# First FFN of a four-layer graph network: four buffers of each kind in the quantisation, and sums of magnitudes as two float32r passes

## The chip, the cores and the metric

One core of a Trainium2 chip runs the whole program in one launch. The metric is the device time of one execution in microseconds (us); of the kernel before it is the median of three runs.

## The reference, cut to what matters

The network alternates four graph layers with four feed-forward layers (FFN) on 625 nodes of 512 features. The change is in the first FFN, which takes the normalised rows x (625x512) and weights that are quantised to three values, scaled by group:

```
def _quantize_weight(w, group_size):           # group_size = 128, EPS = 1e-5
    wg = w.reshape(o, i // group_size, group_size)
    scale = mean(abs(wg), axis=-1, keepdims=True) + EPS
    wq = clip(round(wg / scale), -1.0, 1.0) * scale
gate = x @ quantized(w_gate).T                  # 512 -> 1408
up   = x @ quantized(w_up).T                    # 512 -> 1408
y    = (silu(gate) * up) @ quantized(w_down).T  # 1408 -> 512
```

So for each run of 128 input weights the sum of the magnitudes is needed in full precision, and a weight becomes its sign times the scale if twice its magnitude is over the scale, and 0 otherwise.

## The kernel before, in words

Each engine has its own stream of instructions, written out in order; semaphores join them. The 1408 hidden features are cut into three units u = 0, 1, 2 of 512, 512 and 384 (`WIDTHS`). A unit's three weight matrices lie in WR[(u+1) % 2], so that unit u+1 is loaded and quantised while unit u is multiplied. The load of a unit is queued on SyncE and waits until TensorE is done with the unit before the one it replaces (`weights_used`).

In unit u TensorE (the loop from L1079) does, for each m of the 128-wide parts of the unit, a wide projection with the gate weights and one with the up weights (`project_wide`, matmuls by L732; the first pair of unit 0 by `two_projections`, L1027, between the transposes of the last tiles). ACT takes Silu of the gate half (`gated`, L1739), DVE multiplies it with the up half (L2558). Each frees its PSUM slot; there are two wide slots. Then come five down projections (L1065), whose results DVE adds to the stream (L2176). PSUM slots of kind T, also two, take the sums of magnitudes.

The quantisation of unit u+1 (`quantized`, on each engine a generator) goes in groups: 128 input rows by the unit's width (`groups_of`: 12 groups of 512 columns for unit 1; 8 of 384 and 3 of 512 for unit 2). For one group:

- ACT writes the magnitudes (L1640) and the signs (L1641) of the weights into the buffers AW and SGN. It runs `deep // 2` groups ahead, and waits before it until the product of the group that held the buffer is done (`quant_ready`, L1638).
- TensorE multiplies the magnitudes with a matrix of ones, an fp32 matmul (L915), which sums over the 128 rows.
- ACT copies sum/128 + 1e-5 into SCL (L1651).
- DVE compares 2 x magnitude with the scale (L2402), and multiplies the result with the scale (L2404).
- POOL multiplies this with the sign, back into the weights (L2028). For unit 0 itself, earlier in the program, DVE does this too (L2407).

`deep` is the number of buffers: 3 in the quantisation of unit 0, 2 in those of units 1 and 2. `PACE` says how many groups stand behind each gate and each up projection: in unit 0 one and two, in unit 1 none in the first round (m = 0), then two and two. Each generator is made at a unit's start and advanced by `next(ahead)`.

Of the kernel before, what the change touches and what calls it, by code (L numbers as in the profile page):

```python
# [32 lines left out]
NEG = -1.0e30  # L33
# [154 lines left out]
def program(nc, a, out, loops):  # L188
# [3 lines left out]
    def sb(name, shape, dt=F32):  # L192
        return ctx.enter_context(nc.sbuf_tensor(name, shape, dt))

    def passing(name, shape, dt=F32):

        with nc.sbuf_tensor(name, shape, dt) as t:
            return t

    def sem(name):  # L200
        return ctx.enter_context(nc.semaphore(name))
# [8 lines left out]
    with ctx:  # L210
# [23 lines left out]
        EA2 = sb("EA2", [128, N])  # L234
        with nc.sbuf_tensor("MODW_high", [128, D], F32):
            HRT_HIGH = passing("HRT_HIGH", [128, 4, N + 1], F32R)
        MODW = sb("MODW", [128, 4, D])
        BR = sb("BR", [128, 3, D])
        CS = sb("CS", [128, C_END])
# [41 lines left out]
        HOT0 = passing("HOT0", [128, NT, 4 * P], F32R)  # L281
        with nc.sbuf_tensor("AR_parts", [128, HR_], F32):
            HR = passing("HR", [128, NT, HEADS0, 2, DH0], F32R)
        with nc.sbuf_tensor("AR_hot", [128, HR_ + 2 * NT * D], F32):
            HOT1 = passing("HOT1", [128, NT, 4 * P], F32R)
        with nc.sbuf_tensor("AR_blocks", [128, PR_ + NT * N], F32):
# [4 lines left out]
        def view(at, parts, *shape, dt=F32):  # L291
# [95 lines left out]
        COND4 = view(KT_ + 1905, 128, N)  # L387
        CT8 = view(V_, 8, N)
        ROW0 = [FIRST[:, D * b:D * (b + 1)] for b in range(4)]
        AW = [ROW0[0:3]] + 2 * [[MODW[:, b, :] for b in range(2)]]  # L390
        SGN = [ROW0[3:4] + [WR[:, 0, 1, 1024 + D * b:1024 + D * (b + 1)] for b in range(2)]] + 2 * [[MODW[:, 2 + b, :] for b in range(2)]]
        SCL = [[MODW[:, 0, :], BR[:, 2, :], FS_ROWS[:, 0:D]]] + 2 * [
            [BR[:, 1 + b, :] for b in range(2)]]

        ID = CS[:, C_ID:C_ID + 128]
        SEL = CS[0:8, C_SEL:C_SEL + D]
# [26 lines left out]
        y_ready = sem("y_ready")  # L423
        uv_ready, hr_split = sem("uv_ready"), sem("hr_split")
        terms_ready, row_part_ready = sem("terms_ready"), sem("row_part_ready")
        short_ids_ready, short_ids_out = sem("short_ids_ready"), sem("short_ids_out")
        ids_in = [sem(f"edge_ids_in_{b}") for b in range(2)]
        apart_ready, from_ready, hot_built = sem("apart_ready"), sem("from_ready"), sem("hot_built")
        diff_filled, diff_taken, score_ready = sem("diff_filled"), sem("diff_taken"), sem("score_ready")
        weighed_ready = sem("weighed_ready")  # L430
        scattered = sem("scores_scattered")
        sums_scattered = [sem(f"sums_scattered_{b}") for b in range(2)]
        clear_row_ready, sums_cleared = sem("clear_row_ready"), sem("sums_cleared")
        scores_cleared = sem("scores_cleared")
        keys_ready, totals_ready = sem("keys_ready"), sem("totals_ready")
        onehot_ready, onehot_used = sem("onehot_ready"), sem("onehot_used")
# [12 lines left out]
        head_weighed, prob_ready = sem("head_weighed"), sem("prob_ready")  # L449
        relu_ready = sem("relu_ready")  # L450
        bias_added = sem("bias_added")
        absw_ready, kept_ready, quant_ready = sem("absw_ready"), sem("kept_ready"), sem("quant_ready")
        layer_ready = sem("layer_ready")
        value_rows_free = sem("value_rows_free")
# [34 lines left out]
        def loads(sp):  # L489
# [35 lines left out]
                    sp.dma_start(ER[g % 4][lo:hi].rearrange("p a b -> p (a b)"),  # L525
                                 a["edge_attr"][lo:hi, 256 * g:256 * (g + 1)]).then_inc(edge_in[g % 4], 16)

            sp.wait_ge(clear_row_ready, 2)
            for b in range(2):
                sp.dma_start(pair_sums[b].rearrange("(p q) c -> p (q c)", p=128)  # L530
                             .rearrange("p (a q) -> p a q", a=2),
                             FLAT[1].unsqueeze(1).broadcast_to([128, 2, 3053])).then_inc(sums_cleared, 16)
            sp.wait_ge(short_ids_ready, 1)
            for r in range(2):
                sp.dma_start(short_ids[r].rearrange("(m q) -> m q", q=P), SHORT_IDS[:, r, :])\
                  .then_inc(short_ids_out, 16)
# [173 lines left out]
        def _(pe):  # L710
# [199 lines left out]
            def quantized(u):  # L910

                for k, (j, c, width) in enumerate(groups_of(u)):
                    g = fill("T")
                    pe.wait_ge(absw_ready, n.add(absw_ready))
                    mm(g.ap[:, 0:width], ONES[:, :], AW[u][k % len(AW[u])][:, 0:width], start=True, stop=True)\  # L915
                        .then_inc(g.filled, 1)
                    yield

            ahead = quantized(0)
# [581 lines left out]
        def _(act):  # L1501
# [131 lines left out]
            def quantized(u):  # L1633
                def magnitudes(k):

                    j, c, width = groups[k]
                    if done[0] + k >= deep:
                        act.wait_ge(quant_ready, done[0] + k - deep + 1)  # L1638
                    w = wm((u + 1) % 2, j)[:, c, 0:width]
                    fn(AW[u][k % deep][:, 0:width], w, ACT.Abs).then_inc(absw_ready, 1)  # L1640
                    fn(SGN[u][k % deep][:, 0:width], w, ACT.Sign)  # L1641

                groups, deep = groups_of(u), len(AW[u])
                act.wait_ge(loaded[(u + 1) % 2], n.now(loaded[(u + 1) % 2]) + 48)
                for k in range(deep // 2):
                    magnitudes(k)
                for k, (j, c, width) in enumerate(groups):
                    if k + deep // 2 < len(groups):
                        magnitudes(k + deep // 2)
                    s = take("T")  # L1650
                    fn(SCL[u][k % deep][:, 0:width], s.ap[:, 0:width], ACT.Copy, bias=1e-5, scale=1.0 / 128)\  # L1651
                        .then_inc(s.taken, 1)
                    if k == len(groups) - 1:
                        done[0] += len(groups)
                    yield
# [78 lines left out]
            def gated(m, tiled=False):  # L1734
                s = take("W")
                if tiled:
                    fn(SG[m % 2].rearrange("p (c n) -> p c n", c=NT), by_tile(s), ACT.Silu).then_inc(s.taken, 1)
                else:
                    fn(SG[m % 2], s.across[:, :], ACT.Silu).then_inc(s.taken, 1)  # L1739
# [3 lines left out]
                fn(XT[:, :, tile(t)], s.ap[:, 0:4 * P].rearrange("p (c n) -> p c n", c=K4), ACT.Copy)\  # L1743
                    .then_inc(s.taken, 1)

            transpose_y()
            for u in range(3):
                n.add(loaded[(u + 1) % 2], 48)
                ahead = quantized(u + 1) if u < 2 else iter(())
                for m in range(WIDTHS[u] // 128):  # L1750
                    pace = PACE[u][min(m, 1)]
                    gated(m, tiled=(u == m == 0))
                    for _ in range(pace[0]):
                        next(ahead, None)
                    psum.skip(W=1)
                    for _ in range(pace[1]):
                        next(ahead, None)
                psum.skip(N=NT)
# [367 lines left out]
        def _(dve):  # L2126
# [54 lines left out]
                dve.wait_ge(s.taken, n.now(s.filled))  # L2181


            v.memset(FLAT[1], 0.0).then_inc(clear_row_ready, 1)
            v.memset(FLAT[0], NEG).then_inc(clear_row_ready, 1)
            v.memset(TS[:, :, :], 0.0)
            v.memset(CW[:, :, :], 0.0)
            v.memset(CWP[:, :, 0:1], 1.0)
# [3 lines left out]
            dve.wait_ge(start_done, 10)  # L2192
            dve.wait_ge(index_in, 48)
            v.tensor_copy(SHORT_IDS[:, 0, :], SRC_ROWS)
            v.tensor_copy(SHORT_IDS[:, 1, :], DST_ROWS).then_inc(short_ids_ready, 1)
            v.scalar_tensor_tensor(KEYT, SRC_ROWS, float(N), DST_ROWS, ALU.mult, ALU.add).then_inc(keys_ready, 1)
            v.reduce_max(SM[0:ET, 0:1], WEIGHT_ROWS, AX.X).then_inc(layer_ready, 1)
            dve.wait_ge(keys_ready, 1)
# [195 lines left out]
                    ALU.mult).then_inc(uv_ready, 1)  # L2394
            def quantized(u):

                for k, (j, c, width) in enumerate(groups_of(u)):
                    s = psum.next("T")
                    dve.wait_ge(s[0].taken, s[1])
                    deep = len(AW[u])  # L2400
                    w, z = AW[u][k % deep][:, 0:width], SCL[u][k % deep][:, 0:width]
                    step(v.scalar_tensor_tensor(w, w, 2.0, z, ALU.mult, ALU.is_gt))  # L2402
                    if u:
                        v.tensor_tensor(z, z, w, ALU.mult).then_inc(kept_ready, 1)  # L2404
                    else:
                        step(v.tensor_tensor(z, z, w, ALU.mult))
                        v.tensor_tensor(wm(1, j)[:, c, 0:width], z, SGN[0][k % deep][:, 0:width], ALU.mult)\  # L2407
                         .then_inc(quant_ready, 1)
                    yield
# [153 lines left out]

            psum.skip(T=NT)
            v.tensor_scalar(MASK[:, :, :], CNT[:, :, :], 0.5, -NEG, ALU.is_lt, ALU.mult)
            for u in range(3):
                ahead = quantized(u + 1) if u < 2 else graph_weights()
                for m in range(WIDTHS[u] // 128):
                    pace = PACE[u][min(m, 1)]
                    s, k, _ = psum.next("W")  # L2570
                    for _ in range(pace[0]):
                        next(ahead, None)
                    b = take("W")
                    dve.wait_ge(s.taken, k)
                    gated(m, b, tiled=(u == m == 0))
                    for _ in range(pace[1]):
                        next(ahead, None)
                if u < 2:
                    for t in range(NT):
                        add_to_stream(t, take("N"))  # L2580
                else:
                    followed(streamed, norm_y)
# [522 lines left out]
```

## Time and profile before

| | us |
|---|---|
| median of three runs | 2250.25 |
| lowest and highest | 2247.23, 2251.97 |
| profiled execution | 2255.45 |
| its span | 2253.6 |
| TensorE matmuls busy | 2119.1 (94%) |
| DVE, ACT, POOL busy | 1024.7, 710.9, 551.3 |
| mean granted clock of TensorE | 0.972 |

In the profile, PE is TensorE, PEld its weight loads. An fp32 matmul stands as two instructions, and spans of pipelined matmuls overlap, so the cost of one is read from start to start. A tile is named by the tensor it lies in: AR is the large arena, WR the weights, MODW and BR are small tensors that the quantisation borrows for its buffers.

### The profile page before, as it was taken

How to read it: one execution, taken by the hardware profiler on the slowest of the kernel's cores; microseconds unless marked ns; L12 is line 12 of the kernel's file. 1: busy time of each engine (PE TensorE's matmuls, PEld its weight loads, DVE VectorE, ACT ScalarE, POOL GpSimd, SP SyncE). 2: the span in 40 equal slices, each digit the busy share in tenths (PEclk: the TensorE clock that was granted, in tenths of full speed). 3: DMA queues.
4: the chain of work that ended last, by engine and by line, in shares of the span. 5: the costliest groups of instructions: out<-in, count | busy, mean ns of one | idle time of the engine just before them, and what ended most of it. 6: DMA issues, size and time to landing. Idle time of an engine off the chain costs nothing.

```text
span 2253.6 us, 21932 instructions
## 1 busy us (share of the span) xinstructions
PE 2119.1 (94%) x8162; PEld 1276.7 (57%) x8162; DVE 1024.7 (45%) x2159; ACT 710.9 (32%) x1191; POOL 551.3 (24%) x467
## 2 busy tenths in 40 slices
PE   5899887898889999998999999999999999999998
PEld 3577564787456565554565565565565544444443
DVE  8898677686334324356445355255355300000002
ACT  1477565675231110012242242252251111111110
POOL 4678763453220101012003003002102200122202
PEclk9999999799999789999999999999999899999999
DMA  9522213631112102111011011010101677778832
GB/s 345 178 32 32 27 14 76 171 90 60 41 58 75 38 19 86 43 75 61 15 57 62 19 57 42 30 51 24 53 9 48 246 294 291 295 303 300 300 128 74
DMA packets 61507, 237.47 MB, mean 105 GB/s; under 512 B 23343, under 2 KB 28419, under 8 KB 39276
## 3 DMA queue, kind: packets, MB, share of 16 engines
q1 hardware_dynamic: 31898, 168.25, 20.7%
q0 software_dynamic: 26336, 62.19, 9.0%
q10 hardware_dynamic: 3168, 5.63, 0.7%
q8 instruction: 66, 1.08, 0.2%
q14 instruction: 39, 0.32, 0.0%
HBM read 204.06 MB, written 31.96 MB: 105 GB/s over the span
## 4 chain that ended last, share of the span: by engine, by line
PE 77%; DVE 12%; issue 4%; POOL 3%; ACT 3%; DMA 2%; ACTq 0%; DVEq 0%; POOLq 0%
PE PS L739 10%; PE PS L1027 10%; PE PS L732 9%; PE PS L1420 7%; PE PS L1429 7%; PE PS L1458 7%; PE PS L883 3%; PE PS L1065 3%; PE PS L1306 2%; PE PS L1223 2%; PE PS L1326 2%; PE PS L1327 2%; PE PS L750 1%; PE PS L1205 1%; DVE AR L2436 1%
## 5 line engine op out<-in xcount | busy, mean ns | idle before, releaser
L1984 POOL TENSOR_TENSOR RSTD<-VE,HALF 125x1 f32<-125x1 f32 x100 | 81.1, 811 | 972.5 <-DVE VE L2154 972.5
L1027 PE MATMUL PS<-XT,WR 128*128 128x500 f32 (+2 forms) x992 | 233.5, 392 | 8.4 <-ACT XT L1526 4.4
L883 PE MATMUL PS<-HR,HOT 125*125 125x512 f32 x800 | 211.8, 413 | 16.4 <-DVE HOT L2298 14.9
L2991 DVE TENSOR_TENSOR AR<-AR,PS 128x512 f32<-128x512 f32 (+1 forms) x44 | 30.3, 688 | 404.3 <-PE PS L1429 404.3
L739 PE MATMUL PS<-WR,XT 128*125 128x512 f32 (+1 forms) x464 | 205.5, 590 | 0.6 <-DVE AR L2775 0.3
L1027 PEld LDWEIGHTS PS<-XT,WR 128*128 128x128 f32 x992 | 144.7, 193 | 87.9 <-issue 72.5
L883 PEld LDWEIGHTS PS<-HR,HOT 125*125 125x125 f32 x800 | 147.0, 192 | 58.3 <-DVE HOT L2298 17.2
L2002 POOL DMA_INDIRECT pair_sums<-CW,SIDX x80 | 136.2, 1702 | 54.1 <-DMA pair_sums<-CW,SIDX 21.9
L739 PEld LDWEIGHTS PS<-WR,XT 128*125 128x125 f32 x464 | 86.9, 193 | 89.0 <-issue 85.0
L732 PE MATMUL PS<-XT,WR 128*128 128x313 f32 (+3 forms) x432 | 120.7, 436 | 1.8 <-DVE CW L2262 1.3
L1943 ACT ACTIVATE AR<-PS 128x512 f32<-128x512 f32 (+1 forms) x44 | 26.3, 597 | 299.0 <-PE PS L1420 299.0
L2176 DVE TENSOR_TENSOR AR<-PS,AR 125x512 f32<-125x512 f32 x55 | 38.0, 691 | 178.9 <-PE PS L739 107.3
L732 PEld LDWEIGHTS PS<-XT,WR 128*128 128x128 f32 (+1 forms) x432 | 82.9, 193 | 40.6 <-issue 9.9
L2013 POOL DMA_INDIRECT pair_scores<-TS,SIDX x80 | 88.6, 1107 | 63.0 <-DMA pair_scores<-TS,SIDX 47.5
L732 PE MATMUL PS<-AR 128*125 128x313 f32 (+3 forms) x360 | 101.5, 435 | 0.0
L1526 ACT ACTIVATE XT<-PS 128x500 f32<-128x500 f32 x60 | 35.3, 590 | 209.5 <-PE PS L750 209.5
L1458 PE MATMUL PS<-AR,MODW 128*128 128x512 f32 (+1 forms) x192 | 86.4, 593 | 0.7 <-ACT MODW L1932 0.7
L732 PEld LDWEIGHTS PS<-AR 128*125 128x125 f32 (+1 forms) x360 | 61.1, 187 | 33.9 <-DVE DEN L2813 14.8
L739 PE MATMUL PS<-WR,AR 128*125 128x512 f32 (+1 forms) x200 | 76.6, 530 | 1.7 <-ACT AR L1917 0.9
L2298 DVE SCALAR_TENSOR_TENSOR HOT<-AR,NODE,WR 125x500 fp32r<-125x500 int16 x100 | 71.1, 731 | 7.0 <-ACT WR L1558 6.1
L2319 DVE TENSOR_REDUCE TS<-WR 125x8 f32<-125x512 f32 x80 | 54.4, 680 | 40.3 <-DMA pair_scores<-TS,SIDX 40.3
L1458 PE MATMUL PS<-WR,MODW 128*128 128x512 f32 (+1 forms) x160 | 71.9, 592 | 0.0
(427 smaller groups left out, 3874.2 us busy)
## 6 DMA issues: line engine op xcount, KB each, us to landing
WR<-in_qkv SPq DMA_DIRECT2D x12, 1024.0 KB
WR<-in_omm SPq DMA_DIRECT2D x12, 1024.0 KB
pair_scores<-CNT SPq DMA_DIRECT2D x1, 12212.0 KB
AR<-pair_scores SPq DMA_DIRECT2D x5, 2187.5 KB
AR<-in_x_a SPq DMA_DIRECT2D x10, 1024.0 KB, 9.8
AR<-in_x_b SPq DMA_DIRECT2D x10, 1024.0 KB, 4.9
AR<-in_x_c SPq DMA_DIRECT2D x10, 1024.0 KB, 7.3
WR<-in_x_a SPq DMA_DIRECT2D x8, 1024.0 KB, 8.9
```

Source lines behind the costliest of these rows:

```text
L732: last = mm(s.across[0:parts, c0:c1], lhs(k), rhs(k)[:, c0:c1], start=(k == 0), stop=(k == terms - 1))
L739: last = mm(s.ap[0:P, 0:cols], lhs, rhs, start=(k == 0), stop=(k == len(pairs) - 1))
L883: last = mm(DIFF[m % 4], HOT[g % 2][0:P, k, tile(j)], HR[0:P, k, :, b, :], start=(k == 0 and b == 0), stop=(k == NT - 1 and b == 1))
L1027: last = mm(by_tile(s)[:, t0:t1, :], w[:, k, 128 * m:128 * (m + 1)], XT[:, k, P * t0:P * t1].rearrange("p (c n) -> p c n", n=P), start=(k ...
L1065: last = mm(o.ap[0:P, :], HT[:, m, tile(t)], w[:, m, :], start=(m == 0), stop=(m == len(chunks) - 1))
L1420: last = mm(bank(2 + k % 2, rows_of(k)), stationary(k, c), w[:, c, :], start=(c == 0), stop=(c == K4 - 1))
L1429: last = mm(bank(4 + k % 2, rows_of(k)), stationary(k, c), w[:, c, :], start=(c == 0), stop=(c == K4 - 1))
L1458: last = mm(bank(6 + n % 2, rows), HTX[k % 2][:, c, 0:rows], w[:, c, :], start=(u == 0 and c == 0), stop=((is_shared(k) or u == 1) and c = ...
L1984: g.tensor_tensor(RSTD[:, t:t + 1], VE[:, t:t + 1], HALF[:, :], ALU.pow)\
L2002: g.indirect_dma_start(out=pair_sums[m % 2], out_offset=bass.IndirectOffsetOnAxis(ap=SIDX[:, m:m + 1], axis=0), in_=CW[:, m, :], in_offset ...
L2013: g.indirect_dma_start(out=pair_scores, out_offset=bass.IndirectOffsetOnAxis(ap=SIDX[:, m:m + 1], axis=0), in_=TS[:, m % SCORES_AHEAD, :], ...
L2298: v.scalar_tensor_tensor(HOT[g % 2][0:P, k, :], IDB[g // 2 % 2][0:P, 1, 500 * (g % 2):500 * (g % 2 + 1)], NODE[:, 0, k:k + 1], FROM[q % 4] ...
```

## The change

For the quantisation of units 1 and 2 there are now four buffers of each kind, in the arena, and so ACT runs two groups ahead. ACT writes the magnitudes twice, once in full and once rounded to float32r (the high part); DVE subtracts the rounded from the full one (the low part); TensorE sums both parts into one PSUM slot by two float32r passes in place of the fp32 matmul. Each generator gets a first step of its own that prepares two groups: for unit 1 it is taken on ACT after the third of five transposed tiles and on DVE after the mask, for unit 2 at the start of unit 1's second round, ahead of its Silu and gated product. Two semaphores of the program's start are merged into one.

```diff
+        HIGH_PARTS = passing("HIGH_PARTS", [128, 4, D], F32R)
...
+        with nc.sbuf_tensor("AR_low", [128, 8192], F32):
+            LOW_PARTS = passing("LOW_PARTS", [128, 4, D], F32R)
...
-        AW = [ROW0[0:3]] + 2 * [[MODW[:, b, :] for b in range(2)]]
-        SGN = [ROW0[3:4] + [...]] + 2 * [[MODW[:, 2 + b, :] for b in range(2)]]
+        AW = [ROW0[0:3]] + 2 * [[view(XL_ + D * b, 128, D) for b in range(4)]]
+        SGN = [ROW0[3:4] + [...]] + 2 * [
+            [view(at, 128, D) for at in (10240, 10752, 11264, 12640)]]
         SCL = [[MODW[:, 0, :], BR[:, 2, :], FS_ROWS[:, 0:D]]] + 2 * [
-            [BR[:, 1 + b, :] for b in range(2)]]
+            [BR[:, b, :] for b in range(3)] + [view(XL_ + 4 * D, 128, D)]]
...
# TensorE
-                    mm(g.ap[:, 0:width], ONES[:, :], AW[u][k % len(AW[u])][:, 0:width], start=True, stop=True)\
-                        .then_inc(g.filled, 1)
+                    if u:
+                        for part_ in (HIGH_PARTS, LOW_PARTS):
+                            last = mm(g.ap[:, 0:width], ONES[:, :].bitcast(F32R), part_[:, k % 4, 0:width],
+                                      start=(part_ is HIGH_PARTS), stop=(part_ is LOW_PARTS))
+                    else:
+                        last = mm(g.ap[:, 0:width], ONES[:, :], AW[u][k % len(AW[u])][:, 0:width],
+                                  start=True, stop=True)
+                    last.then_inc(g.filled, 1)
...
# ACT
-                    fn(AW[u][k % deep][:, 0:width], w, ACT.Abs).then_inc(absw_ready, 1)
+                    if u:
+                        fn(AW[u][k % deep][:, 0:width], w, ACT.Abs)
+                        fn(HIGH_PARTS[:, k % deep, 0:width], w, ACT.Abs).then_inc(rounded_ready, 1)
+                    else:
+                        fn(AW[u][k % deep][:, 0:width], w, ACT.Abs).then_inc(absw_ready, 1)
...
                 for k in range(deep // 2):
                     magnitudes(k)
+                if u:
+                    yield
...
-            transpose_y()
+            for t in range(3):
+                turned_row(t)
+            ahead = quantized(1)
+            next(ahead)
+            for t in range(3, NT):
+                turned_row(t)
             for u in range(3):
                 n.add(loaded[(u + 1) % 2], 48)
-                ahead = quantized(u + 1) if u < 2 else iter(())
                 for m in range(WIDTHS[u] // 128):
                     pace = PACE[u][min(m, 1)]
+                    if u == m == 1:
+                        ahead = quantized(2)
+                        next(ahead)
                     gated(m, tiled=(u == m == 0))
...
# DVE
+                def low_part(k):
+                    width = groups[k][2]
+                    dve.wait_ge(rounded_ready, n.add(rounded_ready))
+                    v.tensor_tensor(LOW_PARTS[:, k % 4, 0:width], AW[u][k % 4][:, 0:width],
+                                    HIGH_PARTS[:, k % 4, 0:width].bitcast(F32), ALU.subtract).then_inc(absw_ready, 1)
+                if u:
+                    low_part(0)
+                    low_part(1)
+                    yield
+                for k, (j, c, width) in enumerate(groups):
+                    if u and k + 2 < len(groups):
+                        low_part(k + 2)
...
             v.tensor_scalar(MASK[:, :, :], CNT[:, :, :], 0.5, -NEG, ALU.is_lt, ALU.mult)
+            ahead = quantized(1)
+            next(ahead)
             for u in range(3):
-                ahead = quantized(u + 1) if u < 2 else graph_weights()
+                if u == 2:
+                    ahead = graph_weights()
                 for m in range(WIDTHS[u] // 128):
                     pace = PACE[u][min(m, 1)]
+                    if u == m == 1:
+                        ahead = quantized(2)
+                        next(ahead)
                     s, k, _ = psum.next("W")
```

## Rows read from the trace of the kernel before

**Rows 1.** The page, part 4: the chain that ended last, by engine.
```profile
PE 77%; DVE 12%; issue 4%; POOL 3%; ACT 3%; DMA 2%; ACTq 0%; DVEq 0%; POOLq 0%
```

**Rows 2.** The chain in order of time (start us, us, what), one group in unit 0.
```profile
552.26 1.27 POOL WR L2028
553.56 0.63 ACT MODW L1640
554.19 0.52 ACT MODW L1641
554.71 0.49 ACT BR L1651
555.23 0.70 DVE MODW L2402
555.95 0.70 DVE BR L2404
556.72 1.28 POOL WR L2028
```

**Rows 3.** Busy time by stretch: length, PE, PEld, DVE, ACT, POOL, clock, DMA.
```profile
547.50:595.40 47.90, 37.58 (x128) 23.05 (x127) 16.73 (x25) 21.64 (x39) 12.65 (x10) 1.00 0.00 0
613.00:663.10 50.10, 42.82 (x150) 27.97 (x151) 13.72 (x23) 17.46 (x36) 9.23 (x9) 1.00 0.28 111
```

**Rows 4.** The timeline of PE in units 0 and 1 (start us, us, engine line).
```profile
555.27 4.37 PE L732 MATMUL PS<-XT,WR 128*128 128x312 f32 x16
559.48 1.02 PE L915 MATMUL PS<-MODW,ONES 128*128 128x512 f32 x2
560.34 4.37 PE L732 MATMUL PS<-XT,WR 128*128 128x312 f32 x16
...
595.42 17.33 PE L1065 MATMUL PS<-WR,AR 128*125 128x512 f32 x40
613.01 12.86 PE L732 MATMUL PS<-XT,WR 128*128 128x312 f32 x48 [0.27 <-issue]
...
663.13 17.33 PE L1065 MATMUL PS<-WR,AR 128*125 128x512 f32 x40
```

**Rows 5.** The timeline of PE in the first graph layer: ten float32r matmuls.
```profile
200.10 2.58 PE L883 MATMUL PS<-HR,HOT 125*125 125x512 f32 x10
202.52 0.39 PE L894 MATMUL PS<-Y,WR 125*128 125x512 bf16 x1
```

**Rows 6.** Operations that write float32r: a group of ACT, one of DVE.
```profile
L1664 ACT ACTIVATE HRT_HIGH<-PS 128x500 fp32r<-128x500 f32 x5 | 3.0, 594 | 0.8 <-PE PS L925 0.8
490.68 0.68 DVE L2426 TENSOR_TENSOR LEFT<-PS,LEFT 128x500 fp32r<-128x500 f32 x1
```

**Rows 7.** The timelines of DVE and POOL where they meet.
```profile
596.87 1.65 POOL L2028 TENSOR_TENSOR WR<-BR,MODW 128x512 f32<-128x512 f32 x1 [3.20 <-DVE BR L2404]
663.82 0.80 DVE L2558 TENSOR_TENSOR AR<-AR,PS 128x625 f32<-128x625 f32 x1
663.98 1.27 POOL L2028 TENSOR_TENSOR WR<-BR,MODW 128x512 f32<-128x512 f32 x1 [3.19 <-DVE BR L2404]
664.54 1.26 DVE L2402 SCALAR_TENSOR_TENSOR MODW<-MODW,BR 128x512 f32<-128x512 f32 x1
```

**Rows 8.** DMA rate in 40 slices of 526 to 542 us, and 612 to 628.
```profile
GB/s 0 0 0 20 164 123 246 430 492 389 369 492 410 410 430 430 410 389 492 389 369 512 410 389 338 139 0 20 13 13 0 0 0 0 0 0 0 41 0 0
GB/s 0 0 0 0 164 266 123 348 430 369 512 430 369 492 369 451 451 369 410 369 471 389 430 471 380 21 257 115 115 189 95 142 95 142 95 142 95 189 47 237
```

**Rows 9.** The timeline of ACT: a tile copy, and the Silu of two rounds.
```profile
541.85 0.59 ACT L1526 ACTIVATE XT<-PS 128x500 f32<-128x500 f32 x1 [3.48 <-PE PS L750]
547.48 0.69 ACT L1737 ACTIVATE AR<-PS 128x625 f32<-128x625 f32 x1 [0.79 <-PE PS L1027]
625.91 0.69 ACT L1739 ACTIVATE AR<-PS 128x625 f32<-128x625 f32 x1 [7.72 <-PE PS L732]
```

**Rows 10.** Busy time of one stretch, columns as in rows 3.
```profile
735.00:840.00 105.00, 102.03 (x371) 64.71 (x370) 28.13 (x88) 18.20 (x33) 6.58 (x10) 0.82 0.08 30
```

More of the change, by code:

```diff
@@ L389, in program @@
         ROW0 = [FIRST[:, D * b:D * (b + 1)] for b in range(4)]
-        AW = [ROW0[0:3]] + 2 * [[MODW[:, b, :] for b in range(2)]]
-        SGN = [ROW0[3:4] + [WR[:, 0, 1, 1024 + D * b:1024 + D * (b + 1)] for b in range(2)]] + 2 * [[MODW[:, 2 + b, :] for b in range(2)]]
+        AW = [ROW0[0:3]] + 2 * [[view(XL_ + D * b, 128, D) for b in range(4)]]
+        SGN = [ROW0[3:4] + [WR[:, 0, 1, 1024 + D * b:1024 + D * (b + 1)] for b in range(2)]] + 2 * [
+            [view(at, 128, D) for at in (10240, 10752, 11264, 12640)]]
         SCL = [[MODW[:, 0, :], BR[:, 2, :], FS_ROWS[:, 0:D]]] + 2 * [
-            [BR[:, 1 + b, :] for b in range(2)]]
+            [BR[:, b, :] for b in range(3)] + [view(XL_ + 4 * D, 128, D)]]
         ID = CS[:, C_ID:C_ID + 128]
@@ L425, in program @@
         terms_ready, row_part_ready = sem("terms_ready"), sem("row_part_ready")
-        short_ids_ready, short_ids_out = sem("short_ids_ready"), sem("short_ids_out")
+        short_ids_out = sem("short_ids_out")
         ids_in = [sem(f"edge_ids_in_{b}") for b in range(2)]
@@ L432, in program @@
         sums_scattered = [sem(f"sums_scattered_{b}") for b in range(2)]
-        clear_row_ready, sums_cleared = sem("clear_row_ready"), sem("sums_cleared")
+        first_rows_ready, sums_cleared = sem("first_rows_ready"), sem("sums_cleared")
         scores_cleared = sem("scores_cleared")
@@ L451, in program @@
         bias_added = sem("bias_added")
+        rounded_ready = sem("magnitudes_rounded")
         absw_ready, kept_ready, quant_ready = sem("absw_ready"), sem("kept_ready"), sem("quant_ready")
@@ L526, in edge_rows @@
                                  a["edge_attr"][lo:hi, 256 * g:256 * (g + 1)]).then_inc(edge_in[g % 4], 16)
-            sp.wait_ge(clear_row_ready, 2)
+            sp.wait_ge(first_rows_ready, 2)
             for b in range(2):
@@ L532, in loads @@
                              FLAT[1].unsqueeze(1).broadcast_to([128, 2, 3053])).then_inc(sums_cleared, 16)
-            sp.wait_ge(short_ids_ready, 1)
+            sp.wait_ge(first_rows_ready, 3)
             for r in range(2):
@@ L2181, in add_to_stream @@
                 dve.wait_ge(s.taken, n.now(s.filled))
-            v.memset(FLAT[1], 0.0).then_inc(clear_row_ready, 1)
-            v.memset(FLAT[0], NEG).then_inc(clear_row_ready, 1)
+            v.memset(FLAT[1], 0.0).then_inc(first_rows_ready, 1)
+            v.memset(FLAT[0], NEG).then_inc(first_rows_ready, 1)
             v.memset(TS[:, :, :], 0.0)
@@ L2194, in _ @@
             v.tensor_copy(SHORT_IDS[:, 0, :], SRC_ROWS)
-            v.tensor_copy(SHORT_IDS[:, 1, :], DST_ROWS).then_inc(short_ids_ready, 1)
+            v.tensor_copy(SHORT_IDS[:, 1, :], DST_ROWS).then_inc(first_rows_ready, 1)
             v.scalar_tensor_tensor(KEYT, SRC_ROWS, float(N), DST_ROWS, ALU.mult, ALU.add).then_inc(keys_ready, 1)
@@ L2395, in quantized @@
             def quantized(u):
-                for k, (j, c, width) in enumerate(groups_of(u)):
+                groups = groups_of(u)
+                def low_part(k):
[10 more added lines that the diff above has]
+                        low_part(k + 2)
                     s = psum.next("T")
```

## The prediction

> **What bounds the kernel now.** I read the page's chain of waits first [rows 1]: most of the span is TensorE, but a part goes to DVE, ACT and POOL. The chain in order of time shows where [rows 2]. In the first FFN (units u = 0, 1, 2 of 512, 512 and 384 columns), while unit u is multiplied, the weights of unit u+1 are quantised, and that quantisation is the chain. One group is: absolute value 0.63 and sign 0.52 on ACT, the copy of the sums 0.49, two DVE operations of 0.70, the signed product on POOL 1.28, and then the next absolute value, because there are only two buffers. The period is 556.72 - 552.26 = 4.46 us for each 512-wide group. The table by stretch [rows 3] says the same: TensorE is busy 37.6 of 47.9 us in unit 0 and 42.8 of 50.1 in unit 1, at a granted clock of 1.00. So some 17 us of TensorE's idle time lie here, beside the ones-matmuls themselves. TensorE's own timeline [rows 4] gives its terms: one wide projection is 559.48 - 555.27 = 4.21 us, the fp32 sum of a 512-wide group is 560.34 - 559.48 = 0.86 us (two instructions), and unit 0's down projection starts at 595.42, unit 1's at 663.13. These two starts are what the change can move. What follows in this kernel waits for them, its weight loads included, so I let it move along undiminished.
>
> **TensorE's part.** Removed: an fp32 sum per group. Added: two float32r instructions. No row shows them with the ones matrix; the nearest is the gather, 125x512 float32r, ten instructions in 202.52 - 200.10 = 2.42 us, 0.24 each [rows 5]. I take 0.49 for a 512-wide group and 0.38 for a 384-wide one (0.24 scaled by 384/512, a little rounded up; at most 0.49). The dear end is that float32r of this form costs what fp32 does, 0.86 a pass; that is a rival below.
>
> **ACT's part.** One more absolute value, 0.52 beside its neighbours, written as float32r. ACT writing 128x500 float32r took 0.59 [rows 6], the same as its fp32 copies, so no surcharge. ACT then needs 3 x 0.52 + 0.49 = 2.05 per group.
>
> **DVE and POOL.** One more DVE operation, high subtracted from full: 0.70 like its neighbours (a 500-wide one that writes float32r took 0.68 [rows 6]). DVE then needs 3 x 0.72 = 2.16 per group from start to start. In the old chain DVE and POOL never worked together, now they must. Rows 7 show what happens then: POOL's product ran from 663.98 to 665.25; a DVE product with one PSUM operand beside it took its ordinary 0.80, but the next DVE operation, with both inputs in SBUF, took 1.26, and ended 0.55 after POOL had. The other way round, POOL took 1.65 in place of 1.27. So these two exclude each other, and I add them: 2.16 + 1.27 = 3.43 us per 512-wide group. For 384 columns I scale to 1.75 + 1.0 = 2.75. The cheap end is no exclusion (2.16); the dear end is that POOL only gets in when DVE has nothing: for two groups 2 x (2.16 + 1.27), and 1.04 for ACT's two operations and some 0.2 of handovers, 8.1, or 4.06 a group. I take 3.43, because the rows show whoever asked first being served first.
>
> The Trainium skill, GPSIMD Engine Reference, section Key points, speaks against the change in the same place: POOL "shares its SBUF interfaces with VectorE — contention with DVE instructions in a 2-port perf mode or with two SBUF inputs". It gives no price. Were there no such contention, the gain below would be 26.9 instead of 24.4; all numbers here go by rows 7.
>
> **Unit 0 (12 groups of 512).** Start-up: the weights have landed by 536.4 (the transfer's slices of 0.4 us end with the 26th) [rows 8]. ACT now does both first groups, 6 x 0.52 = 3.1 us, after its third transposed tile, in the idle 3.48 us before its copy at 541.85 [rows 9]: hidden; if not, at most those 3.1 us. DVE's first two subtractions (1.4 us) fit before 547. Silu starts at 547.48 [rows 9]; TensorE is free at about 548.1 and does groups 0 and 1 to 549.1. Group 2 needs the PSUM slot of group 0, which ACT copies only after three operations for group 2: 548.07 + 3 x 0.52 + 0.55 = 550.2. So 1.1 us of stall, sum done 550.7. Then three rounds of gate, 1 sum, up, 2 sums: 3 x (8.42 + 3 x 0.49) = 29.7, end 580.4. Is TensorE ever held? A round lasts 9.9 us, DVE and POOL need 3 x 3.43 + 0.72 for the gated product = 11.0, so they fall behind by 1.1 a round. But a sum needs only the subtraction done two groups ahead, and the slot of the up projection only the gated product of the round before; walking through it operation by operation, the subtraction is 0.2 to 2 us early each time and the last gated product ends at 582.7, before the down projection reaches its fourth part (580.4 + 3 x 0.87 = 583.0). No stall. Down starts at 580.4 in place of 595.42: 15.0 us gained. DVE then still owes two groups, is free for the first addition to the stream only at about 588.0, and the third down tile, ready at 580.4 + 2 x 3.45 = 587.3, waits 0.8 for its PSUM bank. Net 14.2.
>
> **Unit 1 (8 groups of 384, 3 of 512).** The load goes out when unit 0 is done and lands some 9.5 us after unit 1's start [rows 8]; it does so now too. ACT's first two groups (6 operations, 2.6 us) now come ahead of the second round's Silu, which ran at 625.91 [rows 9], 12.9 after the start at 613.01: 9.5 + 2.6 = 12.1, just in time; if late, as much is lost. On the old scale, zero is the end of the second gate projection, 613.01 + 12.86 = 625.9. TensorE's work from there: 5 x 4.21 + 8 x 0.38 + 3 x 0.49 = 25.6. DVE and POOL: four groups a round, 4 x 2.75 + 0.72 = 11.7 against TensorE's 9.9. Walked through, they are late twice: the subtraction of group 9 (about 20.9) holds its sum 0.6 us, and in the last round two groups stand ahead of the gated product, which ends at about 29.7 where the down projection wants it at 28.8: 0.9. Down starts, in effect, at 27.1, in place of 663.13 - 625.9 = 37.2: 10.2 gained. Its additions find DVE free.
>
> **The other edits.** The merged semaphores keep the same producers and the same order of waits: nothing. The new places of the buffers move no instruction. SyncE's queue and POOL's indirect transfers are not passed by any moved step: SyncE waits for the products of unit 0's own weights and for TensorE being done with a unit, both where they were. The moved start on ACT stands ahead of two tile copies, that on DVE ahead of one gated product; both are priced above.
>
> **Sum.** 14.2 + 10.2 = 24.4 us. The profiled execution took 2255.45 (its span 2253.6 and 1.85 around it); it becomes 2231.0. That run lies 5.2 above the median of the three timed ones (2250.25, from 2247.23 to 2251.97); taken from the median, the forecast is 2225.9. I give 2226.
>
> **Rivals.** (a) No exclusion between DVE and POOL: no stalls of 0.8, 0.6, 0.9 and next to no lag, gain 26.9, 2223. For it: nothing but that the overlaps in the trace are few. 5%. (b) POOL starves behind DVE: 4.06 us a group. Unit 0's last subtraction then comes about ten periods after the start, some 6 us later than TensorE wants it, and unit 1 loses as much again with its gated product: gain about 13, 2237. For it: three DVE operations back to back where there were two; against it: POOL's 1.65 [rows 7]. 10%. (c) The change doesn't give cheap sums: two float32r passes over fp32 data cost 2 x 0.86. The stalls vanish into work: unit 0's down starts at 548.1 + 5.2 + 3 x (8.42 + 5.2) = 594.1, 1.3 gained, unit 1's at about 0.6 less: 2248. Against it: rows 5. 4%. (d) Slower: the granted clock. The stretch from 735 to 840 ran at a mean of 0.82 [rows 10], the FFN's at 1.00 [rows 3]. The stretch in question is about 110 us of TensorE's work after the change (units 0 and 1 with their down projections); at 0.82 it lengthens by 110 x (1/0.82 - 1) = 24 us. That is the point from which it decides: any lower, and the kernel is slower than before; at 0.75, 37 us lost, net 12 slower, 2262. Against it: the clock stayed at 1.00 here even with TensorE a fifth idle, and it is now busier. 3%. My forecast, with sizes off by a few us, holds the other 78%.
>
> **How the numbers follow.** The likeliest case alone spans 2220 to 2232: two hidden starts that might cost 3 us each, float32r at up to 0.49 for the narrow groups (1 us), the runs' own spread of 2.5 us to either side. With (a) and (b) the range is 2218 to 2238. About 0.2% (4.5 us) is what a measurement here can tell from no change. Faster takes all but (c), (d) and a little: 0.93; same is (c): 0.04; slower is (d): 0.03.
>
> **What would show it.** Right: in the changed trace no POOL-to-ACT wait on the chain between 548 and 663; down projections that start near 580 and at 27 us after the second gate projection of unit 1; sums of two instructions of about 0.24 us from start to start; DVE operations with two SBUF inputs of up to 1.9 us where POOL works. Wrong: TensorE waiting for the DVE subtraction in every round (then b), 0.86 us from the first pass to the second (c), a granted clock below 1.00 here (d), or a gain that the next stages give back in new waits.

## The result and the profile after

The changed kernel took 2234.24 us (median of 9 runs, 2227.41 to 2241.61), the one before 2257.01 (9 runs, 2247.23 to 2263.81); the ratio is 0.9903, with a 95% interval of 0.9888 to 0.9917, so 21.9 us less (18.7 to 25.3). Forecast were 24.4 us less and a time of 2226 (2218 to 2238). The time came out 8.2 higher; 6.8 of that is the median of the kernel before, which was 2250.25 in three runs and is 2257.01 in nine. The changed kernel's profiled execution took 2236.88 us (2231.0 forecast), its span 2235.0.

The chain of waits of the changed kernel in order of time (start us, us, what), the answer to [rows 2]:

```profile
552.10 0.52 ACT AR L1656
552.61 0.50 ACT BR L1668
553.15 0.74 PE PS L922 x2
553.89 4.21 PE PS L737 x16
558.10 0.46 PE PS L922 x2
558.56 4.21 PE PS L737 x16
562.77 0.93 PE PS L922 x4
563.70 4.21 PE PS L737 x16
...
577.74 0.69 ACT AR L1756
...
582.51 0.81 DVE AR L2597
...
601.39 10.78 DMA WR<-in_down
612.19 0.52 ACT AR L1652
...
615.11 0.58 PE PS L922 x2
615.69 4.21 PE PS L737 x16
619.90 0.69 PE PS L922 x4
620.59 4.21 PE PS L737 x16
```

The cycle ACT, DVE, POOL, ACT is gone. After one short start in each unit, the chain is projection, sums, projection, all on TensorE. Only at the end of unit 0 it passes over ACT and DVE once more, from the last Silu (577.74) to the last gated product (582.51), which a weight load of the down projection waits for; TensorE's matmuls have no idle time there. A sum costs 0.46 us for 512 columns and 0.69 / 2 = 0.35 for 384. Busy time by stretch, columns as in [rows 3]; the first two stretches are unit 0 and unit 1 up to their down projections, the third is one round of unit 0:

```profile
550.40:583.10 32.70, 31.70 (x128) 23.28 (x127) 29.56 (x34) 24.16 (x45) 13.87 (x10) 1.00 0.00 1
600.70:640.00 39.30, 38.35 (x150) 28.11 (x151) 23.89 (x35) 21.77 (x47) 10.25 (x9) 1.00 0.35 141
563.54:573.34 9.80, 9.80 (x40) 7.19 (x39) 9.39 (x12) 7.66 (x15) 4.77 (x4) 1.00 0.01 2
```

TensorE is idle 1.0 us in each stretch, where [rows 3] had 10.3 and 7.3. In the round it is never idle, with DVE at 9.39 of 9.80 us. TensorE's timeline, the answer to [rows 4]:

```profile
547.49 3.74 PE L1038 MATMUL PS<-XT,WR 128*128 128x125 f32 x32
...
553.15 0.50 PE L922 MATMUL PS<-HIGH_PARTS,ONES 128*128 128x512 f32 x1 [1.00 <-ACT BR L1668]
...
583.13 17.33 PE L1076 MATMUL PS<-WR,AR 128*125 128x512 f32 x40
600.72 12.86 PE L737 MATMUL PS<-XT,WR 128*128 128x312 f32 x48 [0.26 <-issue]
613.87 0.42 PE L922 MATMUL PS<-HIGH_PARTS,ONES 128*128 128x384 f32 x1 [0.28 <-DVE LOW_PARTS L2427]
...
615.11 0.41 PE L922 MATMUL PS<-HIGH_PARTS,ONES 128*128 128x384 f32 x1 [0.65 <-DVE LOW_PARTS L2427]
...
640.03 17.33 PE L1076 MATMUL PS<-WR,AR 128*125 128x512 f32 x40
657.62 25.49 PE L737 MATMUL PS<-XT,WR 128*128 128x312 f32 x96 [0.26 <-issue]
```

**A yardstick: one stretch of the trace.** Call S the stretch from the first pair's last 32 matmuls to unit 2's first projection: 657.62 - 547.49 = 110.13 us, and in the kernel before, where those 32 start at 544.60 and unit 2's projection at 680.72, 136.12. The granted clock is 1.00 over S in both of these profiles. It is not in all the runs below, so the table there gives it beside S. So 25.99 us were gained: 15.18 in unit 0 (from S's start to its down projection, 50.82 to 35.64), 10.81 in unit 1 (50.12 to 39.31). The two profiled spans differ by only 18.6, since the changed kernel's profile reached S 2.9 us later and took 1577.4 us behind it instead of 1572.9. That is looked at below. Over S TensorE sat idle 18.1 us before (its matmuls were busy 118.0) and 2.5 us after (107.7).

### The profile page after: what moved, and what is told of

It is laid out like the page before. It is cut to its first block, busy times and chain, and to the rows that moved or that the text cites. A ratio compares the mean times of both kernels' runs of the same rounds, so it can differ in the third digit from the quotient of the medians.

```text
span 2235.0 us, 21978 instructions
## 1 busy us (share of the span) xinstructions
PE 2114.6 (95%) x8162; PEld 1280.8 (57%) x8162; DVE 1049.3 (47%) x2182; ACT 720.5 (32%) x1214; POOL 554.9 (25%) x467
## 3 DMA queue, kind: packets, MB, share of 16 engines
q8 instruction: 66, 1.08, 0.2%
## 4 chain that ended last, share of the span: by engine, by line
PE 78%; DVE 11%; issue 4%; POOL 2%; DMA 2%; ACT 2%; PEldq 0%; PEld 0%; ACTq 0%; SPq 0%; DVEq 0%; POOLq 0%
PE PS L737 11%; PE PS L744 10%; PE PS L1038 10%; PE PS L1431 7%; PE PS L1440 7%; PE PS L1469 7%; PE PS L888 3%; PE PS L1076 2%; PE PS L1317 2%; PE PS L1234 2%; PE PS L1337 2%; PE PS L1338 2%; PE PS L755 1%; PE PS L1216 1%; DMA pair_scores<-TS,SIDX 1%
## 5 line engine op out<-in xcount | busy, mean ns | idle before, releaser
L2026 POOL DMA_INDIRECT pair_sums<-CW,SIDX x80 | 135.6, 1696 | 54.2 <-DMA pair_sums<-CW,SIDX 22.1
L2200 DVE TENSOR_TENSOR AR<-PS,AR 125x512 f32<-125x512 f32 x55 | 38.0, 691 | 179.3 <-PE PS L744 107.7
```

Of the source, the lines that this page charges most:

```text
L2026: g.indirect_dma_start(out=pair_sums[m % 2], out_offset=bass.IndirectOffsetOnAxis(ap=SIDX[:, m:m + 1], axis=0), in_=CW[:, m, :], in_offset ...
```

## The experiments

| run | S | clock over S | TensorE idle in S | unit 0 | unit 1 | time us (runs) | ratio |
|---|---|---|---|---|---|---|---|
| before | 136.12 | 1.00 | 18.1 | 50.82 | 50.12 | 2257.01 (9) | |
| before once more | 136.09 | 0.97 | 14.7 | 50.82 | 50.09 | 2244.22 (1) | |
| changed | 110.13 | 1.00 | 2.5 | 35.64 | 39.31 | 2234.24 (9) | 0.9903 |
| changed once more | 110.13 | 1.00 | 2.4 | 35.65 | 39.30 | 2231.32 (6) | 0.9890 |
| fp32 sums | 115.89 | 1.00 | 0.5 | 39.22 | 41.47 | 2235.26 (6) | 0.9911 |
| two buffers | 150.31 | 0.89 | 26.5 | 57.80 | 55.65 | 2271.38 (6) | 1.0061 |
| three buffers | 129.05 | 0.97 | 16.2 | 44.83 | 49.04 | 2246.66 (1) | |
| four, one ahead | 129.63 | 0.96 | 16.2 | 45.36 | 49.05 | 2251.37 (1) | |
| late start | 118.41 | 0.97 | 7.1 | 40.42 | 42.78 | 2235.22 (1) | |
| narrow product | 110.17 | 1.00 | 2.5 | 35.64 | 39.34 | 2230.16 (1) | |
| subtraction twice | 118.38 | 1.00 | 9.3 | 40.28 | 42.92 | 2224.54 (1) | |
| twice and narrow | 111.72 | 1.00 | 3.8 | 36.14 | 40.40 | 2225.88 (1) | |
| other pace | 113.36 | 1.00 | 4.7 | 37.38 | 40.44 | 2232.39 (6) | 0.9907 |
| signs last | 109.46 | 1.00 | 1.8 | 35.41 | 38.87 | 2229.21 (1) | |

Unit 0 is counted from the start of S to its down projection, unit 1 from its first projection to its down projection. A ratio is to the runs of the kernel before that were taken beside that kernel's (for all but the first they are eleven, with a median of 2255.10). Single times are not compared: look at "subtraction twice", which has the lowest and a long S.

The clock column matters: where the granted clock falls to 0.50, TensorE's matmuls take longer. Over all these profiles fourteen falls to 0.50 lie inside S, and each begins within a wait of TensorE or at most 1.2 us behind one. The waits alone don't bring a fall: the kernel before had the same ones in its first profile, at 1.00 throughout. Where TensorE is not on the chain, a fall costs S nothing: the kernel before once more lost 3.4 us to it, its idle time was 3.4 us shorter, and S stayed at 136.09. Columns as in [rows 3]:

```profile
544.80:680.89 136.09, 121.38 (x384) 70.43 (x383) 43.38 (x64) 42.17 (x79) 27.92 (x27) 0.97 0.10 41
```

**Changed once more.** No edit.

> The changed kernel once more. The measure of all these runs is the stretch S in the trace, from the start of the last 32 matmuls of unit 0's first pair of projections to the start of unit 2's first projection: 136.12 us before (544.60 to 680.72), 110.13 after (547.49 to 657.62), 25.99 gained. Theory: S is again 110.1 within 0.3, because the clock is at 1.00 there, and what the whole execution shows less than 26 of lies elsewhere and changes from run to run: the time lost to the lower clock behind the first FFN was 32 us before and 38 after by the tables of 3 us stretches, and will be anywhere from 31 to 40 here. Rival: the busier FFN makes the clock fall more behind it, always; then 37 or more are lost there in every run of a kernel with the short FFN, and the whole gain stays near 20 us.

S was 110.13 again, the ratio 0.9890 (0.9872 to 0.9908), which is 24.8 us less (20.7 to 28.9).

**fp32 sums.**

```diff
-                        for part_ in (HIGH_PARTS, LOW_PARTS):
-                            last = mm(g.ap[:, 0:width], ONES[:, :].bitcast(F32R), part_[:, k % 4, 0:width], ...)
+                        last = mm(g.ap[:, 0:width], ONES[:, :], AW[u][k % len(AW[u])][:, 0:width], ...)
...
-                        fn(HIGH_PARTS[:, k % deep, 0:width], w, ACT.Abs).then_inc(rounded_ready, 1)
-                    low_part(0)
-                    low_part(1)
-                        low_part(k + 2)
```

> The four buffers and the early start stay, the sums are fp32 matmuls of the full magnitudes again (no high and low part, so one ACT and one DVE operation less a group). Theory (the gain is mostly that the quantisation's chain no longer spans two buffers): S rises by what the sums cost TensorE more, 15 x (0.86 - 0.47) + 8 x (0.65 - 0.35) = 8.3, less about 1 for shorter starts, to 117.5 (116 to 119). Rival (the cheap sums bring most of it): S of 125 or more.

S = 115.89, a little below the range. An fp32 sum costs 0.86 us, as before; all stalls at the starts went too (1.0 and 0.9). In unit 1 no subtraction stands between the magnitudes and the sum any more; in unit 0 ACT's copy comes behind two operations instead of three, and TensorE's first sums last longer. So of 25.99 us, buffers, distance and early start alone bring 20.2, the two passes on top of them 5.8.

**Two buffers.**

```diff
-        AW = [ROW0[0:3]] + 2 * [[view(XL_ + D * b, 128, D) for b in range(4)]]
+        AW = [ROW0[0:3]] + 2 * [[view(XL_ + D * b, 128, D) for b in range(2)]]
...
-                    if u and k + 2 < len(groups):
-                        low_part(k + 2)
+                    if u and k + 1 < len(groups):
+                        low_part(k + 1)
```

SGN, SCL and the parts likewise, and the generators are made at the units' starts.

> The float32r sums alone: two buffers of each kind, one group ahead, and the generators start where the kernel before starts them. Theory: the chain through two buffers stays and gets one more ACT operation, 0.52 (0.41 for 384 columns) a group: about 10 x 0.52 + 6 x 0.41 + 2 x 0.52 = 8.7 more, less 1 for the last sums: S about 144 (141 to 147), slower than before by some 0.35%. Rival (cheap sums): S = 136.1 - 8.3, 128.

The ratio is 1.0061 (1.0039 to 1.0084): the float32r sums alone make the kernel slower, and the cheap-sums rival falls. The chain of this kernel, in unit 0:

```profile
572.70 1.29 POOL WR L2044
574.01 0.63 ACT AR L1652
574.64 0.52 ACT HIGH_PARTS L1653
...
576.20 0.70 DVE AR L2431
576.92 0.70 DVE BR L2433
577.69 1.28 POOL WR L2044
```

The old cycle with the new ACT operation in it: 577.69 - 572.70 = 4.99 us, against 4.46. S = 150.31 is above the range (141 to 147); it grew by 14.2 instead of 8. Two things stood nowhere in my sum. The first is the subtraction, which now lies between ACT and a sum wherever TensorE waits for one: the first two sums of unit 0 wait 1.74 and 0.86, and from the tenth product to the down projection it is 606.85 - 602.97 = 3.88 us, where it was 595.42 - 592.41 = 3.01. The second is the clock:

```profile
549.05:699.36 150.31, 123.80 (x384) 76.28 (x383) 58.11 (x87) 53.08 (x102) 28.01 (x27) 0.89 0.09 37
```

At 0.89 over S, unit 0's down projection takes 626.13 - 606.85 = 19.28 us in place of 17.59, so 1.7 of the 14.2 are the clock's. In unit 0's rounds it adds little: the projections take up to 6.3 us in place of 4.21, yet POOL's products, which mark the cycle, stay 4.98 to 4.99 apart, but for one gap of 5.34. What S would be at 1.00 was not measured; that the cycle is longer, 4.99 against 4.46, does not hang on the clock.

**Late start.** On ACT:

```diff
-            for t in range(3):
-                turned_row(t)
-            ahead = quantized(1)
-            next(ahead)
-            for t in range(3, NT):
+            for t in range(NT):
                 turned_row(t)
...
-                    if u == m == 1:
-                        ahead = quantized(2)
-                        next(ahead)
                     gated(m, tiled=(u == m == 0))
+                    if (u, m) in ((0, 0), (1, 1)):
+                        ahead = quantized(u + 1)
+                        next(ahead)
```

> As the changed kernel, but the generators' first step is taken late: for unit 1 behind all five tile copies and the first Silu on ACT, for unit 2 behind the second round's Silu. Theory: the early start is worth what TensorE would wait at each start: three operations before sum 0, and seven before the copy that sum 2 needs, about 3.0 in unit 0, and 1.8 in unit 1: S about 115 (113 to 116). Rival (the start is hidden by the depth anyway): 110 to 111.

S = 118.41, 8.3 above the changed kernel and above the range (113 to 116). The three waits at unit 0's start are 1.74, 0.85 and 1.04 (1.00 in the changed kernel), the two at unit 1's are 2.29 and 0.65 (0.28 and 0.65): 4.6 more, the 5 expected. Most of the rest is the clock, which fell to 0.50 once in each unit, with TensorE at work and at most 0.4 us idle:

```profile
550.90:554.30 3.40, 3.40 (x8) 2.33 (x7) 3.37 (x5) 2.61 (x6) 1.27 (x1) 0.50 0.00 0
615.80:619.20 3.40, 2.97 (x7) 2.27 (x8) 2.46 (x6) 3.32 (x9) 0.43 (x1) 0.50 0.31 134
```

Half of 2 x 3.4 us is 3.4, and no wait of TensorE follows in either unit in which it could vanish. So the early start is worth about 5 us.

**Three buffers, and four with one ahead.** First `range(3)` and `k % 3` in all places with `low_part(k + 1)` (three buffers); then four buffers as in the change, but:

```diff
-                for k in range(deep // 2):
+                lead = 1
+                for k in range(lead):
...
-                    if k + deep // 2 < len(groups):
-                        magnitudes(k + deep // 2)
+                    if k + lead < len(groups):
+                        magnitudes(k + lead)
...
-                        low_part(k + 2)
+                        low_part(k + 1)
```

> Three buffers of each kind, and ACT and the subtraction only one group ahead in place of two. Theory: the chain is still broken (about 2.5 us a group), but the second sum behind each up projection now needs a subtraction that DVE only reaches after the gated product of the same round, 0.7 + 0.7 less 0.47, some 0.9 us in each of six rounds: S about 115 (112 to 118). Rival (only the number of buffers counts, three are enough): 110 to 111. Rival (four are needed): over 120.

> Four buffers of each kind, but ACT and the subtraction only one group ahead. The run with three buffers had S = 129.05 where 115 was expected. Theory: the distance ahead did that, not the number of buffers: two sums stand back to back on TensorE, and one group ahead ACT begins the second one's magnitudes only behind the round's Silu; then S is 129 here too (126 to 130). Rival (the third buffer's wait for the product was the chain): S 110 to 118.

The first missed: 129.05 instead of 115. With the fourth buffer back, S is 129.63, and TensorE's idle time in it is the same 16.2 us; the 0.6 between them is no more than the clocks, 0.97 and 0.96, can make. So at one group ahead the fourth buffer brings nothing, and at four buffers the second group ahead brings the 19.5 us to 110.13, of which up to 5 are the clock's (129.63 x 0.04). Whether three buffers would do at two ahead was not run. ACT, DVE and TensorE of the kernel with four buffers and one ahead, in unit 1 (three answers):

```profile
642.89 0.69 ACT L1757 ACTIVATE AR<-PS 128x625 f32<-128x625 f32 x1 [3.72 <-PE PS L737]
643.48 0.51 ACT L1652 ACTIVATE AR<-WR 128x384 f32<-128x384 f32 x1
643.89 0.51 ACT L1653 ACTIVATE HIGH_PARTS<-WR 128x384 fp32r<-128x384 f32 x1
```

```profile
644.44 0.56 DVE L2428 TENSOR_TENSOR LOW_PARTS<-AR,HIGH_PARTS 128x384 fp32r<-128x384 f32 x1 [3.13 <-ACT HIGH_PARTS L1653]
```

```profile
645.14 0.42 PE L922 MATMUL PS<-HIGH_PARTS,ONES 128*128 128x384 f32 x1 [1.94 <-DVE LOW_PARTS L2428]
```

ACT idles 3.72 us in front of Silu, which waits for the gate projection; only behind it, in its program, come the magnitudes of the second sum that TensorE wants right after that projection. This order on ACT was missing from my expectation of 115, which had DVE's order only.

**Narrow product.**

```diff
-                    g.tensor_tensor(w, SCL[u][k % deep][:, 0:width], SGN[u][k % deep][:, 0:width], ALU.mult)
+                    g.tensor_tensor(w[:, 0:8], SCL[u][k % deep][:, 0:8], SGN[u][k % deep][:, 0:8], ALU.mult)
```

> POOL's product is done on 8 columns only (the rest of the signed product is left out), so that POOL hardly ever holds the interface it shares with DVE. Theory: DVE's holds of about 1.07 us go, DVE ends each round earlier, and TensorE gains nothing, since it never waited for it: S 110.1 within 0.4. Rival (the exclusion is on the path): 107 to 109.

S = 110.17. DVE's 512-wide operations all take their plain 0.69 us now (the gated product 0.80), so the holds were POOL's doing, and TensorE gains nothing: the exclusion is off the path.

**Subtraction twice, and twice with the narrow product.**

```diff
+                    step(v.tensor_tensor(LOW_PARTS[:, k % 4, 0:width], AW[u][k % 4][:, 0:width],
+                                         HIGH_PARTS[:, k % 4, 0:width].bitcast(F32), ALU.subtract))
```

> Each subtraction of the high part is done twice, 0.7 us of DVE more a group, which is 2.2 a round in unit 0 and 2.3 in unit 1. Theory: DVE with POOL was at 9.3 us of a round of 9.8, so it now falls behind by about 1.7 a round in unit 0 and more in unit 1; the slack of the last gated product (some 3 us in unit 0, 0.8 in unit 1) is used up: S 116 (113 to 120). Rival (DVE is busy less than half of the kernel and has room): 110 to 111.

> Subtraction twice, as in the run that had S = 118.38, and POOL's product on 8 columns only (the rest of the signed product is left out). Theory: DVE and POOL exclude each other, and near the edge that decides: without POOL's holds DVE needs some 9.1 us of a round of 9.8, so only the later starts are left, S 111.6 (110.8 to 113). Rival (it was the doubled subtraction's own latency): S stays at 117 to 119.

118.38, then 111.72, both as expected. A round of unit 0 with the doubled subtraction lasts 571.26 - 560.07 = 11.19 us on TensorE's timeline, and busy time by stretch (columns as in [rows 3]) has DVE at 10.99 of such 11.20:

```profile
561.20:572.40 11.20, 10.06 (x40) 7.11 (x39) 10.99 (x15) 7.17 (x14) 4.58 (x3) 1.00 0.01 1
```

Take POOL's holds away and 6.7 of the 8.3 us come back. So the exclusion costs nothing where DVE is busy 9.4 of 9.8 us a round, and 6.7 us of S with one more operation of 0.7 us a group.

**Other pace.**

```diff
-PACE = (((1, 2), (1, 2)), ((0, 0), (2, 2)), ((1, 2), (1, 2)))
+PACE = (((0, 2), (2, 2)), ((0, 0), (1, 3)), ((1, 2), (1, 2)))
```

> Another spread of the groups over the rounds: unit 0 two in the first round and then two behind each gate and up projection, unit 1 one and three. Theory: the 1.0 us that sum 2 waited for its PSUM slot goes, and the 0.65 of unit 1's second sum: S 108.5 (107.5 to 109.5), the whole execution 25 to 28 us below the kernel before, not to be told from the changed kernel by time. Rival (four groups in a round are too much for DVE and POOL in unit 0, 12.4 against 10.3 us): S of 110 or more.

S = 113.36, the rival was right (the 1.00 at unit 0's start did go): four groups in a round of unit 0 put DVE and POOL over TensorE's time, and three sums in a row in unit 1 wait too. The ratio 0.9907 (0.9885 to 0.9930) can't be told from the changed kernel's.

**Signs last.**

```diff
-                    fn(SGN[u][k % deep][:, 0:width], w, ACT.Sign)
...
                         .then_inc(s.taken, 1)
+                    if u and k + 2 < len(groups):
+                        signs(k + 2)
```

> A version that should beat both: as the changed kernel, but ACT does the sign of a group behind the copy of the sums, and at a start behind both groups' magnitudes. Theory: 0.5 us less before sum 2 of unit 0, 0.4 less before the second sum of unit 1: S 109.2 (108.9 to 109.6). Rival (the copy comes earlier but DVE is at the subtraction then): 110.1. The time can't be told from the changed kernel's.

S = 109.46, 0.67 us better than the change and the best of all by the trace. One run says nothing of its time.

**Before once more.** No edit.

> The kernel before once more, for its trace. Theory: S is again 136.1, since its chain is made of fixed durations; ahead of the stretch and behind it the times without the clock's losses are 516 to 520 and 1538 to 1540 us as in all other traces, and what the clock takes behind it lies between 21 and 39 us. Rival (a shorter FFN loses more to the clock behind it): under 30 here.

Now to the 4.5 us behind S. I summed (1 - granted clock) over stretches of 3 us, which is the time that the lower clock takes; limits differ a little from the ones in my expectation, and so do the sums.

| profile | behind S | taken by the clock | rest |
|---|---|---|---|
| before / once more | 1572.9 / 1561.5 | 34.3 / 22.1 | 1538.6 / 1539.4 |
| changed / once more | 1577.4 / 1574.6 | 39.1 / 34.4 | 1538.3 / 1540.2 |
| fp32 sums / signs last | 1574.0 / 1573.3 | 36.5 / 34.0 | 1537.5 / 1539.3 |
| two buffers / three | 1573.0 / 1572.8 | 33.4 / 33.6 | 1539.6 / 1539.3 |
| subtraction twice / twice and narrow | 1561.6 / 1561.4 | 21.5 / 22.4 | 1540.1 / 1539.1 |

The rest is constant within 2.8 us in these ten profiles (summed over the clock's own records instead of rounded stretches, within 1.7 us in all fourteen), the clock's part goes from 21.5 to 39.1, and both kinds of FFN have a 22. That the shorter FFN always loses more is refuted. Ahead of S the profiles lie between 541.8 and 552.0, likewise without an order. So the profiled pair's 18.6 us instead of 26.0 is within what single executions scatter by. Whether the medians hide a give-back of 1 to 3 us is not settled: 26.0 lies inside the second interval (20.7 to 28.9), just outside the first (18.7 to 25.3).

## Why the prediction was right, point by point

- **What bounds.** Right: two buffers and the ACT-DVE-POOL chain. Undoing buffers, distance and early start together gives more than the whole loss back, S = 150.31; of these, the second group ahead is worth 14 to 19.5 us and the early start about 5.
- **TensorE's part.** 0.49 and 0.38 a group forecast, 0.46 and 0.35 measured; two passes at fp32 price (c) did not come. Nor did a lower clock in S (d): 1.00 in both profiles of the changed kernel.
- **Unit 0.** Down projection 15.0 us earlier forecast, 15.18 measured, with the one stall named there (1.1; it is 1.00). The 0.8 in the third down tile did not come: DVE began its first addition at 587.44, 39.95 after the start of S, where I had 43.4.
- **Unit 1.** 10.2 forecast, 10.81 measured, but partly by luck, for two errors nearly cancel. The two late waits, 0.6 and 0.9, did not come. The start, held for just in time, was late: the weights were there for ACT at 612.19, 11.5 us after the unit's start at 600.72, where I had read 9.5 from the rates of [rows 8]. Packet by packet, 381 of the load's 384 packets of 8192 bytes had ended 9.4 us after the unit's start, in both traces; the last three ran one after another and ended at 10.9, among the packets of the next transfer, where a rate can't show them, and ACT began 0.6 later. So 10.9 stood in the trace of the kernel before. TensorE lost 0.28 + 0.65 us.
- **DVE and POOL.** The step that was mis-sized: 3.43 us a group and 11.0 a round forecast, against 9.29 from one gated product to the next (573.03 - 563.74), with a wait for ACT in it. So DVE never fell behind TensorE's 9.80, and the three stalls of 0.8, 0.6 and 0.9 that followed from falling behind did not come. Their lines in one round, the answer to [rows 7] (DVE, then POOL):

```profile
563.74 0.80 DVE L2597 TENSOR_TENSOR AR<-AR,PS 128x625 f32<-128x625 f32 x1
564.46 1.27 DVE L2427 TENSOR_TENSOR LOW_PARTS<-AR,HIGH_PARTS 128x512 fp32r<-128x512 f32 x1
565.65 0.68 DVE L2441 SCALAR_TENSOR_TENSOR AR<-AR,BR 128x512 f32<-128x512 f32 x1
566.37 0.69 DVE L2443 TENSOR_TENSOR BR<-BR,AR 128x512 f32<-128x512 f32 x1
566.98 0.68 DVE L2427 TENSOR_TENSOR LOW_PARTS<-AR,HIGH_PARTS 128x512 fp32r<-128x512 f32 x1
567.58 1.77 DVE L2441 SCALAR_TENSOR_TENSOR AR<-AR,BR 128x512 f32<-128x512 f32 x1
...
573.03 0.80 DVE L2597 TENSOR_TENSOR AR<-AR,PS 128x625 f32<-128x625 f32 x1
```

```profile
563.90 1.28 POOL L2052 TENSOR_TENSOR WR<-AR 128x512 f32<-128x512 f32 x1 [1.35 <-DVE AR L2443]
567.13 1.67 POOL L2052 TENSOR_TENSOR WR<-BR,AR 128x512 f32<-128x512 f32 x1 [1.95 <-DVE BR L2443]
573.20 1.28 POOL L2052 TENSOR_TENSOR WR<-BR,AR 128x512 f32<-128x512 f32 x1 [1.36 <-DVE BR L2443]
```

The exclusion is there as forecast, and each side serves the one who asked first. But a hold costs DVE 1.77 - 0.69 = 1.08, and only 0.58 where the gated product, with its PSUM operand, runs beside POOL; POOL's starts lie 573.20 - 563.90 = 9.30 us apart over a round. I had counted 1.27 three times and the gated product on top. Rival (a), no exclusion, would also give no stalls: TensorE can't tell the two apart, DVE's durations and the narrow product do. (Its 26.9 is 0.2 more than its terms, 24.4 + 0.8 + 0.6 + 0.9 = 26.7.) That the gain of S, 25.99, lies nearer to that rival than to 24.4 comes from the mis-sized step, not from a missing exclusion. Rival (b) did not come: POOL waited for one operation at most.
- **Downstream.** That the rest moves along undiminished is right for everything but the clock, whose spread over single executions (some 17 us) is larger than my range allowed for one run, though not for a median.

The forecast gain of 24.4 lies within the measured interval and 1.6 under what S shows. The exclusion was seen rightly but counted too dear (2.3 us of stalls that did not come), and the late weights (0.93) made up for part of it.

## What to carry to other kernels

When a chain through several engines sets the pace, count its operations per period and the number of groups it spans: here the new ACT operation lengthened the cycle by its full 0.52 us while two buffers closed it, and TensorE's round not at all when four buffers opened it. That holds only while every engine's work in a round fits TensorE's: one DVE operation more a group cost 8.3 us. More buffers need distance to pay: the producer must be ahead by as many groups as the consumer takes back to back, and ahead in its own program, in front of any instruction that waits for the consumer. Compare kernels by a stretch of the trace, and look at its clock first: at 1.00 in both it resolves 0.1 us where medians of whole runs need 4, and at 0.97 it gave the late start 8.3 us in place of 5.

## What the runs showed of the hardware

DVE operations with both inputs in SBUF and POOL's product run one after the other (1.77 and 1.27 us in place of 0.69), one with a PSUM operand doesn't (0.80 beside POOL). Without POOL's product the same operations take 0.69. A float32r pass of 128x512 costs TensorE 0.23 us, and the switch from fp32 matmuls to it no measurable time. The kernel before lost 34.3 us to the lower clock behind S in one execution and 22.1 in another, 12.2 apart, where the two spans lie 11.2 apart. A fall of the clock to 0.50 costs its half wherever TensorE is the chain (late start, 3.4 us), and nothing where it waits (the kernel before once more). Of a load of 3 x 1024 KB the last three packets ended 1.5 us after the 381 others.
